# Attention part of a gated block: small matrices turned in row tiles, four phases a batch, other hand-over points

## What is computed

```python
x = x + jnp.tanh(g_xattn[0]) * _L0_xattn_ref(ctx_1024, ctx_1024, _layernorm(x, axis=-1), mask, ...)
# in _L0_xattn_ref, with B=32 batches, S=112 rows of x, S2=375 rows of context, E=256, H=16 heads, D=16:
qh = _split_heads(q @ wq + bq)
kh = _split_heads(k @ wk + bk)
vh = _split_heads(v @ wv + bv)
logits = jnp.einsum('bhqd,bhkd->bhqk', qh, kh) / jnp.sqrt(jnp.float32(D)) + mask * -1000000000.0
attn = jax.nn.softmax(logits, axis=-1)
out = jnp.einsum('bhqk,bhkd->bhqd', attn, vh)
return out @ wo + bo
```

## Time and profile before

| | us |
|---|---|
| median of 3 runs | 1252.23 (1251.17 to 1255.26) |
| the profiled execution | 1245.54 |
| its span | 1243.8 |
| PE busy in the span | 1188.9 |
| start of the second half (first gate matmul, L1139, on PE) | 635.68 |

### The profile page before, as it was taken

How to read it: one execution, slowest core, us unless ns; L and a number is a source line. 1 busy time by engine, 2 the same in 40 slices (tenths; PEclk the granted TensorE clock), 3 DMA queues, 4 the chain that set the end, 5 groups by cost and what they waited for, 6 DMA issues and landing times. The chain is left out here.

```text
span 1243.8 us, 41871 instructions
## 1 busy us (share of the span) xinstructions
PE 1188.9 (96%) x16568; PEld 947.7 (76%) x16568; DVE 902.1 (73%) x2556; ACT 620.0 (50%) x1481; POOL 550.7 (44%) x821
## 2 busy tenths in 40 slices
PE   5699999999999999999879999999999999999995
PEld 4477777777777777777557888888888888888874
DVE  3477777777877777777757877777877777787763
ACT  3366666666666666665434444434444444443431
POOL 3476777677777767777611122122122212212120
PEclk9899999999999999999999999999999999999998
DMA  8899998888778878877315656656666665665663
GB/s 229 193 203 199 207 201 201 178 187 185 179 179 186 183 177 186 178 175 159 69 50 127 163 140 145 152 140 149 148 157 142 137 167 145 142 155 139 148 149 94
DMA packets 263010, 200.31 MB, mean 161 GB/s; under 512 B 195934, under 2 KB 243872, under 8 KB 258720
## 3 DMA queue, kind: packets, MB, share of 16 engines
q1 hardware_dynamic: 262816, 197.64, 70.2%
HBM read 125.49 MB, written 72.11 MB: 159 GB/s over the span
## 5 line engine op out<-in xcount | busy, mean ns | idle before, releaser
L899 POOL TENSOR_SCALAR shifted<-raw,neg_max 112x375 f32<-112x375 f32 x512 | 327.3, 649 | 163.5 <-DVE neg_max L781 120.3
L781 DVE CUSTOM_DVE_ANT_0 raw<-bank_s,maskb 112x375 f32<-112x375 f32 x512 | 266.6, 544 | 103.0 <-issue 87.8
L686 ACT ACTIVATE probsT<-bank_t 128x512 f32<-128x512 f32 (+3 forms) x512 | 189.1, 458 | 104.1 <-PE bank_t L460 104.1
L447 PE MATMUL bank_s<-K_stack,Q_stack 128*112 128x375 bf16 x512 | 150.8, 335 | 5.0 <-DVE neg_max L781 4.7
L1444 DVE TENSOR_REDUCE max<-bank_s 112x4 f32<-112x448 f32 x128 | 78.8, 615 | 71.6 <-PE bank_s L1201 71.6
L460 PEld LDWEIGHTS bank_t<-ident,shifted 48*128 48x128 f32 (+1 forms) x3072 | 105.3, 139 | 27.8 <-issue 24.2
L460 PE MATMUL bank_t<-ident,shifted 48*128 48x48 f32 (+1 forms) x3072 | 122.6, 226 | 0.0
L1537 POOL TENSOR_TENSOR mix_bd<-pm_te,tok 128x448 f32<-128x448 f32 x32 | 31.5, 986 | 200.5 <-DMA pm_te<-pm_dram 200.5
L1153 PE MATMUL bank_ab<-xnT,wq2T 128*128 128x224 f32 x512 | 109.4, 357 | 0.7 <-ACT qT L1337 0.6
L1153 PE MATMUL bank_ab<-xnT,wk2T 128*128 128x224 f32 x512 | 109.6, 357 | 0.0
L203 POOL TENSOR_SCALAR var_eps<-moments 112x1 f32<-112x1 f32 x32 | 7.2, 224 | 227.0 <-DVE moments L199 226.8
(11 more groups left out here) (147 smaller groups left out, 2191.8 us busy)
## 6 DMA issues: line engine op xcount, KB each, us to landing
K_stack<-k_dram SPq DMA_DIRECT2D x64, 562.5 KB, 7.8
k_dram<-k_parts SPq DMA_DIRECT2D x32, 562.5 KB, 4.4
att_dram<-att_q SPq DMA_DIRECT2D x31, 511.0 KB, 3.9
att_th<-att_dram SPq DMA_DIRECT2D x31, 511.0 KB, 4.3
v_dram<-mv SPq DMA_DIRECT2D x32, 455.0 KB, 6.5
v<-v_dram SPq DMA_DIRECT2D x32, 455.0 KB, 4.0
K_stack<-k_dram SPq DMA_DIRECT2D x32, 375.0 KB, 9.2
Q_stack<-q_dram SPq DMA_DIRECT2D x64, 168.0 KB, 9.1
```

Source lines behind the costliest of these rows:

```text
L447: nc.tensor.matmul(bank_s[h % 2][0:S, 0:S2], Q_stack[:, p, h, :], K_stack[:, p, h, :], start=True, stop=True).then_inc(scores_ready, 1)
L686: act.activation(probsT[:, g % 2, first_u:end, lo:hi], bank_t[0:KP, bank, column:column + (end - first_u) * (hi - lo)].rearrange("p (u q) ...
L781: dve.tensor_tensor_reduce(raw[:, g % 2, j, :], bank_s[h % 2][0:S, 0:S2], c.maskb[:, :], -1.0, -LEAST, ALU.add, ALU.min, neg_max[:, g % 2, ...
L899: pool.tensor_scalar(shifted[:, g % 2, j, 0:S2], raw[:, g % 2, j, :], -1.0, neg_max[:, g % 2, j:j + 1], ALU.mult, ALU.add).then_inc(shift_ ...
```

## The change

It rewrites the order of the first half on PE, ACT, DVE and POOL:

- Context, x and both turns of the heads are now done by `turn_halves`: two transposes of 64 rows each in the place of one of 112 or 128 rows, into the two banks of `bank_ab`. `xn` and `heads` get 128 partitions, of which the last 16 are zero.
- These pairs stand directly ahead of (or, for `heads_back`, behind) the row tiles of `turn`. The order of a batch has four phases: full-array work, row tiles, column tiles.
- Context and x are turned three batches ahead instead of two; scores 0 to 3 of a batch stand in the body before it.
- `bank_ab` is handed over at other points: `heads_turn` waits for `v_copied`, `turn_ctx` for `x_done` and `v_copied`, the second value step for `outT_copied`, the first for `heads_done`, `heads_back` for `k_copied` and `q_copied`, the second key tile for the copies of the first.
- On SP the query stores stand ahead of the key store, and on DVE the query split stands earlier in the batch. `wo` is loaded in four pieces, with its rows in the order of the new `heads`.
- The gate and projection matmuls that open the second half move within the last bodies.

The core of the diff (removed lines are left out except in `exchange`):

```diff
@@ -340,12 +334,12 @@
             def exchange(b, p, i):
                 by_partition = lambda t: t.rearrange("a q (t p) n -> p (a q) t n", p=P)
-                sp.wait_ge(k_split, b + 1)
-                sp.dma_start(by_partition(k_dram[bass.ds(b, 1)]), k_parts[:, p, :, :, :]).then_inc(k_stored[p], 16)
                 sp.wait_ge(q_split, b + 1)
                 sp.dma_start(by_partition(q_dram[bass.ds(b, 1), 0:PARTS]), q_parts[:, :, :, :]).then_inc(q_stored[p], 16)
                 sp.dma_start(by_partition(q_dram[bass.ds(b, 1), PARTS:Q_COPIES]), q_parts[:, 0:Q_COPIES - PARTS, :, :]).then_inc(q_stored[p], 16)
-                if not (isinstance(b, int) and b < 2):
+                sp.wait_ge(k_split, b + 1)
+                sp.dma_start(by_partition(k_dram[bass.ds(b, 1)]), k_parts[:, p, :, :, :]).then_inc(k_stored[p], 16)
+                if b >= 2:
                     sp.wait_ge(scores_ready, H * (b - 1))
                 sp.wait_ge(k_stored[p], 16 * i + 16)
                 for j, n, first in STACKED:
...
         def _(pe):
...
+            def turn_halves(columns, width, src, f):
+                for r in range(2):
+                    rows = slice(r * HALF, (r + 1) * HALF)
+                    last = nc.tensor.transpose(bank_ab[0:f.stop - f.start, r, columns:columns + width], src[rows, f], c.ident[rows, rows])
+                return last
+            def turn_ctx(b):
+                p, i = b % 2, b // 2
                 pe.wait_ge(ctx_loaded[p], 32 * i + 32)
...
+                if 0 < b < 3:
+                    pe.wait_ge(q_copied, (EC + 1) * b)
+                elif b >= 3:
                     pe.wait_ge(v_copied, 2 * (b - 1))
...
+                if b > 3:
+                    pe.wait_ge(x_done, b - 3)
                 for e in range(EC):
                     for k in range(KC):
...
@@ -487,37 +492,36 @@
                 pe.wait_ge(headsT_copied, b + 1)
                 for g in range(NG):
...
+                    last = turn_halves(g * HALF, HALF, headsT, slice(g * S, (g + 1) * S))
                 last.then_inc(heads_ready, 1)
             def heads_turn(b):
                 pe.wait_ge(heads_done, b + 1)
...
+                flat_heads = heads[:, :, :, :].rearrange("s r h d -> s (r h d)")
                 for e in range(EC):
...
+                    last = turn_halves(e * HALF, HALF, flat_heads, slice(e * P, (e + 1) * P))
                 last.then_inc(outT_ready, 1)
             def project(b):
                 pe.wait_ge(outT_copied, b + 1)
                 for e in range(EC):
...
+                    last = nc.tensor.matmul(bank_ab[0:S, 0, 0:E], outT[:, e, 0:S], c.wo[:, e, :], start=(e == 0), stop=(e == EC - 1))
                 last.then_inc(y_ready, 1)
             def open_x(e):
...
+            def body(b):
+                p = b % 2
+                back = b > 0
+                S_ = lambda n, *hs: [scores(n, n % 2, n // 2, h, n == 0) for h in hs if n < B]
+                S_(b, 4, 5)
+                if b + 2 < B:
+                    keys(b + 2, 0, 0)
+                S_(b, 6)
+                if b + 2 < B:
+                    queries(b + 2)
+                elif b + 2 == B:
+                    open_gates(0)
+                S_(b, 7)
+                turn(b, 0, b == 0)
                 if back:
                     weigh(b - 1, 1 - p, NG - 1, False)
...
+                S_(b, 8, 9)
+                if b + 2 < B:
+                    keys(b + 2, 1, 0)
+                S_(b, 10, 11)
+                turn(b, 1, b == 0)
                 if back:
...
+                    if b + 2 < B:
+                        pe.wait_ge(k_copied, 2 * EC * (b + 3))
+                        pe.wait_ge(q_copied, (EC + 1) * (b + 3))
+                    else:
+                        pe.wait_ge(o.gates_copied, 1)
+                        pe.wait_ge(o.xt_copied, b + 3 - B)
                     heads_back(b - 1)
...
+                weigh(b, p, 0, b == 0)
+                S_(b, 12, 13)
+                if b + 1 < B:
+                    if back:
+                        pe.wait_ge(heads_done, b)
+                    else:
+                        pe.wait_ge(k_copied, 2 * EC * (b + 3))
+                        pe.wait_ge(q_copied, (EC + 1) * (b + 3))
                     values(1 - p, 0)
                     values(1 - p, 1).then_inc(va_ready, 1)
...
+                S_(b, 14, 15)
+                if back:
+                    if b + 1 < B:
+                        pe.wait_ge(v_copied, 2 * b + 3)
+                    heads_turn(b - 1)
+                turn(b, 2, False)
+                weigh(b, p, 1, False)
+                S_(b + 1, 0, 1)
+                if b + 1 < B:
+                    if back:
+                        pe.wait_ge(outT_copied, b)
+                    values(1 - p, 2).then_inc(vb_ready, 1)
                 else:
...
+                    open_proj(0)
+                S_(b + 1, 2)
                 if back:
                     project(b - 1)
...
+                S_(b + 1, 3)
+                if b + 1 == B:
+                    open_proj(1)
+                if b + 3 < B:
+                    turn_ctx(b + 3)
+                    turn_x(b + 3)
+                elif b + 1 < B:
+                    open_x(b + 3 - B)
+                turn(b, 3, False)
+                weigh(b, p, 2, False)
...
+                dve.scalar_tensor_tensor(xb, bank_ab[0:S, 0, 0:E], c.tanh_g[:, 0:1], xb, ALU.mult, ALU.add).then_inc(x_done, 1)
+            def body(b):
+                p = b % 2
+                back = b > 0
+                x_next = b + 3 - B
+                score_max(b, b == 0, 4, 5)
+                if x_next < 0:
+                    moments_of(b + 3)
+                elif x_next < 2:
+                    o.moments_of(dve, c.X[0:S, x_next, :], x_next)
+                score_max(b, b == 0, 6, 7)
+                if x_next < 0:
+                    normalise_x(b + 3)
+                elif x_next < 2:
+                    o.normalise_x(dve, c.X[0:S, x_next, :], x_next)
+                if b + 2 < B:
+                    query_rest(b + 2)
+                score_max(b, b == 0, 8, 9)
+                if b + 2 < B:
+                    split_rest(b + 2)
+                score_max(b, b == 0, 10, 11)
+                if back:
+                    normalise(b - 1)
+                score_max(b, b == 0, 12, 13)
+                if b + 1 < B:
                     value_copy(b + 1, 1 - p, 0)
...
+                score_max(b, b == 0, 14, 15)
+                if b + 2 < B:
+                    key_third(b + 2, p)
+                if b + 1 < B:
+                    score_max(b + 1, False, 0, 1)
+                    value_copy(b + 1, 1 - p, 1)
+                    score_max(b + 1, False, 2)
+                if back:
                     residual(b - 1)
...
+                if b + 1 < B:
+                    score_max(b + 1, False, 3)
             def copy_weights(*numbers):
```

More of the change, by code:

```diff
@@ L529, in open_proj @@
                 last.then_inc(o.proj_ready, 1)
-            def body(b, p, i, first, ahead, last):
-                back, front = not first, not last
-                S_ = lambda *hs: [scores(b, p, i, h, first) for h in hs]
-                if ahead:
-                    transposes(b + 2, i + 1, p)
-                S_(0, 1)
-                if back:
-                    weigh(b - 1, 1 - p, NG - 2, False)
-                    turn(b - 1, NG - 1, False)
-                S_(2, 3)
-                if ahead:
-                    keys(b + 2, p, 0)
-                S_(4)
+            def body(b):
[12 more added lines that the diff above has]
+                turn(b, 0, b == 0)
@@ L628, in _ @@
             pe.wait_ge(v_copied, 2)
-            batches(pe, body)
-            weigh(B - 1, 1, NG - 2, False)
-            open_proj(0)
-            turn(B - 1, NG - 1, False)
+            for h in range(G):
+                scores(0, 0, 0, h, True)
+            for b in range(B):
+                body(b)
             weigh(B - 1, 1, NG - 1, False)
-            pe.wait_ge(o.xt_copied, 2)
+            pe.wait_ge(x_done, B - 1)
             heads_back(B - 1)
-            open_proj(1)
             heads_turn(B - 1)
@@ L881, in _ @@
             key_third(1, 1)
[L882 removed]
+            query_rest(1)
+            split_rest(1)
+            moments_of(2)
             copy_weights(*range(7, len(turns), 2))
[L884 removed]
+            normalise_x(2)
+            score_max(0, True, 0, 1, 2, 3)
+            for b in range(B):
+                body(b)
             dve.wait_ge(o.consts_done, 2)
@@ L951, in _ @@
                 add_bias(b)
-            batches(pool, body)
+            inverse_deviation(2)
+            add_bias(2)
+            shift(0, 0, True)
+            for b in range(B):
+                body(b)
 def switch(nc, z, d, c):
```

313 lines of the change are left out of this document (128 added, 185 removed).

## The result

| | before | changed |
|---|---|---|
| median, us | 1253.7 (1251.17 to 1255.26, 4 runs) | 1288.92 (1284.09 to 1291.54, 4 runs) |
| profiled execution, its span, us | 1245.54, 1243.8 | 1286.45, 1284.3 |
| ratio | | 1.029, 95% interval 1.025 to 1.033 |

The changed kernel is slower, by 35 us in the medians and 40.9 in the profiled executions, where +13.9 was forecast; 1289 lies above the range's upper end of 1279. The sign, the period and two of the three waits came out as worked out. The rest of the time comes from places the sum had at 1 us or at nothing.

The account below looks back on a forecast made before the run. PE, busy 96% of the span, bounds the kernel. Period 18.07 less 0.71 saved plus waits 0.59, 0.48 and 0.12 gives 18.55: +0.48 us 29 times, +13.9, start and end cancelling; 1266 us, range 1257 to 1274 (far ends 1247 to 1279).

Parts of the forecast that it names:

- Savings on PE: Per batch on PE: 64-row pairs replace full-array turns, -0.61 us, and one tiling change fewer, -0.1 us.
- Turn of the heads behind `v_copied`: PE waits 0.59 us a batch ahead of the heads' turn for DVE's copies of the values.
- context's turn behind `x_done`: PE waits 0.48 us a batch ahead of context's turn for DVE's addition after the projection.
- The third, 0.12 for `k_copied`: PE waits 0.12 us a batch ahead of the back turn of `headsT` for ACT's second key copy.
- Rivals 1 and 2: First: hand-overs cost less than tiles save, 1249 or 1232, chance 0.14; second: 64-row pairs don't overlap, 1284, chance 0.04.
- "+1 us" at the start: Start of the kernel: key store issued behind both query stores delays the first stacks' loads by 1 us, between 0 and +2.5.
- Rival 3: Stacks land after the next batch's scores want them; each us over costs 29, 1295 for one us; chance 0.04.
- the stacks come late: The stacks' round trip of store, issues and landing overruns the scores' start; 1295 for one us over, chance 0.04.
- Six issues of some 0.42: SP's issue of the stack loads between key store and landing, part of a 16.0 us round trip.
- The earlier query store helps.: On SP, issuing the query stores sooner was said to help the stacks land in time; no size given.
- End of the first half: Four projection matmuls move earlier from between the last heads' two turns: -1 us, between -3 and +1.
- the stacks' 2.5 us to spare: Store 4.4, issues and landing 9.1 make 16.0 us against a period of 18.5, leaving 2.5 us spare.

Follow-up runs that it names:

- the swaps: Changed kernel with the third or the fourth turn of scores put ahead of the turn that waited: 1304.3 and 1302.5 us; both together 1303.7 us.
- x_early: Changed kernel with SP issuing the x load for batches 4 to 7 ahead of batch 2's stores and stack loads: 1300.7 us, ratio 1.022.
- start_and_stores: Changed kernel with the early x load for batches 4 to 7 and the key store ahead of the query stores in every batch: 1293.0 us, ratio 1.014.
- the pair on one chip: Kernel before and changed kernel, both unedited, profiled again later on the same chip: 1270.5 and 1308.6 us, ratio 1.032.

## Why the prediction missed the size

- **Savings on PE, -0.61 a batch, -0.71 with the changes of tiling.** Nearly as worked out. Context 0.40 for 0.38, x 0.12 for 0.13, turn of the heads 0.17 for 0.13, back turn 0.37 where 0.25 was taken for four pairs; that one has the change to column tiles in it. Without its two waits a period is 18.51 - 1.04 = 17.47, so 0.60 were saved and not 0.71.
- **Turn of the heads behind `v_copied`, 0.59, and context's turn behind `x_done`, 0.48.** Measured 0.53 and 0.51 in every batch, and the swaps showed that the waits are what costs. The third, 0.12 for `k_copied`, did not come. The period was forecast at 18.55 and is 18.51; that it fits this well is in part luck, as the savings came out 0.11 too large in the sum and the waits, 1.19 for 1.04, 0.15 too large.
- **Rivals 1 and 2.** The hand-overs did not cost less than the tiles save: two waits of 1.04 us in sum against some 0.6 saved. And pairs of 64 and 64 rows do run side by side, at 0.066 us.
- **"+1 us" at the start.** This step failed, and most. It looked at the key store alone: context of batch 2 was indeed turned 2.4 us later (46.11 for 43.67), of which 0.3 was left by head 4 of batch 0 (49.80 for 49.48). The x load was not walked. DVE's statistics were moved by a body, which moves the load they need, and SP's queue had it behind nine DMAs of batch 2. x_early gives 11 us for that load's place, and with the order of the stores put back as well (start_and_stores) batch 2 starts 13.4 us earlier. So where +1 was in the sum, these profiles have +14.7, and +9.4 in the pair on one chip.
- **Rival 3, "the stacks come late", at 0.04.** It happened in part, and its sum was short in two places. "Six issues of some 0.42" are 3.4 us (383.86 to 387.26 on SP in the changed kernel) and not 2.5, so that by the page's medians the way from store to last landing is 4.4 + 3.4 + 9.4 = 17.2 us, and 1.3 of the 18.5 were spare and not 2.5. And the store's 4.4 is a median over all batches. In batches 4 to 10, where the x groups lie in the same queue, the store took longer already before the change (the kernel before, 96 to 210):

```profile
DMA to landing us min/median/max: 4.2/6.4/6.8
```

With 6.4 in its place the sum is 19.2, over the 18.5, before the order of the stores is looked at. The kernel before had room for that, as it issued the key store 20.6 us ahead of the batch's first score (314.08 and 334.71 for batch 16), where the changed kernel has 18.3 (342.68 and 360.93).
- **"The earlier query store helps."** The reverse. It is ahead of the key store in the DMA engines; with the order undone (113 to 245) the key store takes 5.0 us in the median, against 7.0, 7.0 and 7.4 in the three profiles of the changed kernel (113 to 230).
- **End of the first half**, -1 and two more periods at +0.48: -1.8 and -2.7 measured.
- **Second half, no term.** +8.0 in the first pair of profiles, +1.5 in the pair on one chip, of which the first gate matmuls at the lower clock are 1 us. That the other 6.5 are differences between runs rests on these two pairs alone.
- **Stops of PE at issue**, which the trace of before has not in this length, were not foreseeable from its rows. In the middle stretch of the first pair they are 2.0 us and of the later one 4.6, before what the lower clock adds.

So two steps failed: the +1 us at the start, and the stacks' 2.5 us to spare, which put batches 2 to 12 at their 4.8 us (measured +11.2 and +17.9, with the stops of PE in it). The range was drawn from the waits and savings alone. It had no room for a queue that wasn't walked.

## What to carry to other kernels

When work is prepared one batch further ahead, list every wait in it, the one-time loads first, and find the DMA's place in the issuing queue: a load that is in time for one body can be late for the one before it. Of two stores in one queue, the one whose data others wait for goes first, even if the other is ready sooner. A median over the whole kernel hides the batches in which a DMA is slow; look at the stretch where it has least room. An order with waits taken away should be judged by the slack of its slowest round trip: here both swaps gave little until the stacks had room, and with it the same savings made a kernel 0.7% faster than the one before (some 3% faster than the changed kernel, by ratios from different chips).

## What the hardware showed that I had not expected

- PE stood 0.7 to 4.25 us with no semaphore open, each time with a packet of the instruction queue begun 2.4 to 3.2 us before it went on; most such packets pass without a stop.
- A stop costs more than its length: behind 10.82 us without work the granted clock is 0.58 over 10 us, and behind 1.55 us 0.71.
- The second half of the kernel before took 608 us in one profile and 633 in a later one; its medians of the two occasions are some 17 us apart too.
- Row tiles of the two halves of the array do not start in the order of the program: a tile of x for the lower half started at 329.80, before two tiles of context for the upper half at 329.86 and 329.92 that stood ahead of it.
